# Attention output with stationary values on four column strips, in a fused AdaLN, attention and mixture kernel

## The reference

```python
Q = (X @ Wq).reshape(n, s, NUM_GROUPS, HEADS_PER_GROUP, KEY_WIDTH)
K = (X @ Wk).reshape(n, s, NUM_GROUPS, KEY_WIDTH)
V = (X @ Wv).reshape(n, s, NUM_GROUPS, VALUE_WIDTH)
raw = jnp.einsum('bsgwe,btge->bstgw', Q, K * scale)
attn = jax.nn.softmax(raw, axis=2)
A = jnp.einsum('bstgw,btge->bsgwe', attn, V).reshape(n, s, NUM_HEADS * VALUE_WIDTH)
P = A @ Wpost
return X + P
```

## Time and profile before

| quantity | value |
|---|---|
| median of 3 runs | 577.44 us (577.16 to 578.15) |
| the profiled execution's own time | 579.19 us |
| its span, first to last instruction | 577.4 us |
| PE busy | 559.4 us (97%) |
| DVE busy | 457.8 us (79%) |
| ACT busy | 390.7 us (68%) |
| POOL busy | 310.5 us (54%) |

### The profile page before, as it was taken

The page is one execution under the profiler, slowest core; times in us unless marked ns, Lnnn a source line. Parts: engine busy times, 40 slices in busy tenths (PEclk is TensorE's granted clock), DMA queues, the critical chain, the costliest instruction groups (busy, mean ns, idle before and its releaser), DMA issues.

```text
span 577.4 us, 14607 instructions
## 1 busy us (share of the span) xinstructions
PE 559.4 (97%) x4408; PEld 475.4 (82%) x4408; DVE 457.8 (79%) x966; ACT 390.7 (68%) x911; POOL 310.5 (54%) x268
## 2 busy tenths in 40 slices
PE   8999999999999999999999999999999998978997
PEld 8888888888888888888888888888888976655664
DVE  4244889898889898989898989898989857862865
ACT  1766777777777777777777777777777535647883
POOL 1102666666666666666666666666666544401950
PEclk9999999999999999999999999999999989989999
DMA  7400000000000000000000000000000000000004
GB/s 239 98 2 2 1 2 2 1 0 0 0 0 0 0 0 0 0 0 0 0 0 0 0 0 0 0 0 0 0 0 0 2 1 0 1 1 2 1 1 145
DMA packets 9367, 7.22 MB, mean 13 GB/s; under 512 B 1088, under 2 KB 8832, under 8 KB 9216
## 3 DMA queue, kind: packets, MB, share of 16 engines
q1 hardware_dynamic: 9344, 6.94, 4.1%
HBM read 4.84 MB, written 2.10 MB: 12 GB/s over the span
## 4 chain that ended last, share of the span: by engine, by line
PE 81%; DVE 8%; ACT 5%; issue 3%; DVEq 1%; POOL 0%; ACTq 0%; POOLq 0%
PE bank_a L692 18%; PE misc L699 10%; PE misc L815 10%; PE bank_t L682 8%; PE bank_s L667 6%; PE misc L706 5%; PE misc L833 3%; PE bank_t L677 3%; PE bank_t L931 3%; PE misc L835 2%; DVE row_max L296 2%; DVE h_max L412 2%; PE bank_s L939 2%; PE misc L939 2%; PE bank_s L807 1%
## 5 line engine op out<-in xcount | busy, mean ns | idle before, releaser
L1346 POOL TENSOR_TENSOR pair<-kx 128x1152 f32<-128x1152 f32 x32 | 82.2, 2568 | 172.5 <-DVE shifted L417 155.7
L692 PE MATMUL bank_a<-v,prob 128*128 128x65 f32 x1024 | 128.7, 274 | 1.2 <-ACT prob L985 0.6
L692 PEld LDWEIGHTS bank_a<-v,prob 128*128 128x128 f32 x1024 | 122.0, 192 | 6.0 <-ACT prob L985 3.0
L1341 POOL TENSOR_TENSOR mix_hi<-mix_hi 128x512 f32<-128x512 f32 (+2 forms) x96 | 116.0, 1208 | 7.5
L296 DVE TENSOR_REDUCE row_max<-bank_s 128x4 bf16<-128x512 f32 x128 | 88.8, 694 | 26.6 <-PE bank_s L667 25.7
L985 ACT ACTIVATE prob<-bank_t 128x512 f32<-128x512 f32 x128 | 68.9, 589 | 8.4 <-PE bank_t L682 6.3
L699 PE MATMUL misc<-yT,wq_sb 128*128 128x128 f32 x512 | 69.8, 279 | 0.8 <-DVE yT L477 0.8
L985 ACT ACTIVATE attT<-misc 128x512 f32<-128x512 f32 x64 | 38.1, 595 | 42.8 <-PE misc L706 42.8
L682 PE MATMUL bank_t<-qT,kT 64*128 64x256 f32 x512 | 66.6, 380 | 0.0
L699 PEld LDWEIGHTS misc<-yT,wq_sb 128*128 128x128 f32 x512 | 62.0, 191 | 4.1 <-DVE yT L477 1.0
L307 DVE TENSOR_TENSOR att<-bank_a,recip_den 128x256 f32<-128x256 f32 x128 | 54.4, 425 | 13.0
(11 more groups left out here) (178 smaller groups left out, 989.1 us busy)
## 6 DMA issues: line engine op xcount, KB each, us to landing
out<-acc_all SPq DMA_DIRECT2D x8, 256.0 KB, 2.3
x_all<-in_xT SPq DMA_DIRECT2D x1, 1024.0 KB, 8.9
w_sb<-in_w SPq DMA_DIRECT2D x2, 512.0 KB
x_all<-in_xT SPq DMA_DIRECT2D x1, 768.0 KB, 6.8
wq_sb<-in_wq SPq DMA_DIRECT2D x1, 512.0 KB, 4.9
wpost_sb<-in_wpost SPq DMA_DIRECT2D x1, 512.0 KB, 9.6
x_all<-in_xT SPq DMA_DIRECT2D x1, 256.0 KB, 3.4
b_rows<-in_b SPq DMA_DIRECT2D x16, 4.0 KB
```

The costliest lines, as they stand in the source:

```text
L692: last = mm(att_bank(g)[:, w, :], prob[:, g % 2, w, :], v1[:, j, g, :], start=(w == 0), stop=True, skip_group_check=True)
L1341: G.tensor_tensor(mix_hi[:, jd, 0:r, :], mix_hi[:, jd, 0:r, :], mix_hi[:, jd, r:2 * r, :], ALU.add).then_inc(s_hi, 1)
L1346: G.tensor_tensor(pair[:, :, :], bass.AP(kx2, jc * 2 * P, [[4 * P, P], [0, SHIFTS], [1, P]]), bass.AP(kx2, jc * 2 * P, [[4 * P, P], [MD, S ...
```

## The change

The roles in stage B are exchanged. The values become stationary, 32 columns of them at a time, and the exponentials move, 512 columns (4 heads x 128 queries) in one matmul. The four groups g write to the four 32-partition strips of one bank, which are four column strips of the array. Two such rounds (`attend(s, j, part)`) give the two halves of the 64 values in `bank_a[0]` and `bank_a[1]`, transposed as the post projection wants them. A third round with 32 columns of ones gives the denominators in a new bank `bank_d`, copied over the 32 partitions of each strip. VectorE inverts them in one instruction of 512 columns and multiplies twice with 512 columns, straight into `attT`. The 16 narrow matmuls, the 8 transposes, the two copies by ScalarE, the 4 short reciprocals and the 4 products of 256 columns go away. `prob` gets four buffers in place of two. One bank less is left for `misc`, so other results move to other banks. The rows of Wpost are permuted on the way in.

Other edits come with it. The sum over eight rows of `mix_lo`, which was three additions (L450, L459, L461), becomes one reduction of 1024 to 128 columns, as in the drain before (L514). The order of the instructions of a slot is new on TensorE, VectorE and ScalarE: the fourth `heads_max` of a batch moves into the same slot as the other three, and the post projection is split in two halves, each issued when its half of `attT` is there.

```diff
-        prob = sb("prob", [P, 2, HPG, P])
-        recip_den = sb("recip_den", [P, 2, HPG])
-        att = sb("att", [P, HEADS, KEY])
+        prob = sb("prob", [P, GROUPS, HPG, P])
+        inv_den = sb("inv_den", [P, HPG, P])
...
+        bank_d = pb("bank_d", [P, HPG, P])
+        misc = [pb(f"misc{i}", [P, QUAD, P]) for i in range(2)]
...
-            def invert(s, g):
-                dve.wait_ge(s_av_mm, 4 * s + g + 1)
-                need(dve, s_att, 4 * s + g - 1)
-                V.reciprocal(recip_den[:, g % 2, :].unsqueeze(2), att_bank(g)[:, :, KEY:KEY + 1]).then_inc(s_rden, 1)
...
+            def invert_den(s):
+
+                dve.wait_ge(s_den_mm, n(s))
+                need(dve, s_attT, 2 * s)
+                V.reciprocal(inv_den[:, :, :], bank_d[:, :, :]).then_inc(s_rden, 1)
+
+            def normalise(s, part):
+
+                dve.wait_ge(s_av_mm, 2 * s + part + 1)
+                dve.wait_ge(s_rden, n(s))
+                need(dve, s_post_mm, s)
+                V.tensor_tensor(attT[:, HPG * part:HPG * (part + 1), :],
+                                bank_a[part][:, :].rearrange("p (w q) -> p w q", q=P), inv_den[:, :, :],
+                                ALU.mult).then_inc(s_attT, 1)
...
+                def row_sum():
+                    dve.wait_ge(s_lo, 4 * d + 1)
+                    V.tensor_reduce(mix_part[:, :], mix_lo[:, :, :].rearrange("p r f -> p f r"), AX.X,
+                                    ALU.add).then_inc(s_lo, 3)
...
+            def denominators(s):
+
+                pe.wait_ge(s_prob, 4 * n(s))
+                for g in range(GROUPS):
+                    rows = slice(32 * g, 32 * (g + 1))
+                    last = mm(bank_d[rows, :, :], ones[:, 0:32], prob[:, g, :, :], start=True, stop=True,
+                              skip_group_check=True)
+                last.then_inc(s_den_mm, 1)
+
+            def attend(s, j, part):
+
+                for g in range(GROUPS):
+                    rows = slice(32 * g, 32 * (g + 1))
+                    last = mm(bank_a[part][rows, :], v[:, j, g, 32 * part:32 * (part + 1)],
+                              prob[:, g, :, :], start=True, stop=True, skip_group_check=True)
                 last.then_inc(s_av_mm, 1)
...
+            def posts(b, part):
+
+                pe.wait_ge(s_attT, 2 * b + part + 1)
+                for k in range(4 * part, 4 * part + 4):
+                    last = mm(bank_d[:, 0, :], wpost_sb[:, k, :], attT[:, k, :],
+                              start=(k == 0), stop=(k == CHUNKS - 1))
+                if part == 1:
+                    last.then_inc(s_post_mm, 1)
```

More of the change, by code:

```diff
@@ L156, in build, with key_out, mix_out @@
         bank_a = [pb(f"bank_a{i}", [P, 512]) for i in range(2)]
-        misc = [pb(f"misc{i}", [P, QUAD, P]) for i in range(3)]
+        bank_d = pb("bank_d", [P, HPG, P])
+        misc = [pb(f"misc{i}", [P, QUAD, P]) for i in range(2)]
         bank_x = [b[:, :].rearrange("p (t f) -> p t f", f=P) for b in bank_a] + [misc[1][:, :, :]]
-        bank_e = [bank_s, misc[2]]
+        bank_e = [bank_s, bank_d]
         bank_b = bank_x[0:2] + [misc[0][:, :, :], misc[1][:, :, :]]
-        def att_bank(g):
-            return bank_a[g % 2][:, 0:HPG * (KEY + 1)].rearrange("p (w e) -> p w e", e=KEY + 1)
+        def key_out(b):
+            return misc[1][:, 0:1, :] if s_is(b, BATCH - 1) else bank_x[1][:, 0:1, :]
+        def mix_out(b):
+            return bank_d[:, 0, :] if isinstance(b, int) and b >= BATCH - 3 else misc[1][:, 0, :]
         s_ld_mod, s_ld_modw, s_ld_x0, s_ld_x, s_ld_qkv = (sem("ld_mod"), sem("ld_modw"), sem("ld_x0"),
@@ L448, in loop_slot @@
-                    if D:
[L449 to L461, removed]
@@ L793, in slot @@
-                if s_is(s, BATCH - 1):
-                    gate_logits(parts_early[1])
-                if s_is(s, BATCH):
-                    pe.wait_ge(s_neg, BATCH)
-                    pe.wait_ge(s_rt, ROUTE_STEPS["count1"])
-                    mm(bank_s[:, 0, 0:EXPERTS], ones[:, :], count[:, :], start=True, stop=True).then_inc(s_cnt1_mm, 1)
-                if A:
-                    if C:
-                        pe.wait_ge(s_attT, 2 * c + 1)
-                    need(pe, s_q, 2 * a)
-                    queries(a, 1)
@@ L850, in slot, with keys, keys_turned @@
[L850 to L854 removed]
+                final = s_is(s, BATCH - 1)
+                def keys(b):
+                    pe.wait_ge(s_x1s, n(b))
+                    mm(key_out(b)[:, 0, :], modw_sb[:, 1, :], x1s[:, :], start=True, stop=True).then_inc(s_kx_mm, 1)
+                def keys_turned(b):
+                    pe.wait_ge(s_kxT, n(b))
+                    nc.tensor.transpose(key_out(b)[:, 0, :], kxT[:, :], ident[:, :]).then_inc(s_kxn_mm, 1)
@@ L855, in slot, with drain_slot @@
+                def drain_slot():
+                    if s == BATCH:
+                        posts(c, 0)
+                        posts(c, 1)
+                        keep_going(6)
+                        pick()
+                        pe.wait_ge(s_ld_ffn, 16 * (3 + P // EXPERTS))
+                        ahead_hidden(0)
+                        pe.wait_ge(s_tok, d)
+                        keys(c)
+                        ahead_hidden(1)
+                        keys_turned(c)
                         pe.wait_ge(s_x1T, n(c))
-                    if s_is(s, BATCH):
@@ L857, in slot @@
                         ahead(0, 1, 2)
-                    if s_is(s, BATCH + 1):
+                        mixing_turned(d)
+                        ahead(3)
+                        tokens_made(d)
+                    if s == BATCH + 1:
                         ahead(4, 5, 6)
-                    if s_is(s, BATCH + 2):
+                        mixing_turned(d)
+                        ahead(7)
+                        tokens_made(d)
+                    if s == BATCH + 2:
                         ahead(8)
@@ L906, in slot @@
-                if s_is(s, BATCH + 2):
-                    ahead_hidden(11)
-                    gate_logits(RECENT[-1:])
-                    ahead(10, 11)
+                        mixing_turned(d)
+                        ahead_output(9)
+                        tokens_made(d)
+                        ahead_hidden(11)
+                        gate_logits(RECENT[-1:])
+                        ahead(10, 11)
+                if isinstance(s, int) and s >= BATCH:
+                    drain_slot()
+                else:
+                    loop_slot()
```

384 lines of the change are left out of this document (171 added, 213 removed).

## The result

The changed kernel takes 722.2 us (median of 4 runs, 721.5 to 724.0) against 577.8 us: the ratio is 1.248, 95% interval [1.245, 1.252]. The forecast was 697 us in a range of 648 to 740: the direction and the mechanism hold, and the clock's term is too small. The narrower range that the forecast gave its own mechanism, 675 to 720 us, is missed by 2 us.

What follows compares the result with a forecast made beforehand. A circle through TensorE and VectorE was taken to bound each slot at 17.0 us: 577.4 + 81 (28 slots) + 2 (slots 1 and 2) + 36 (lowered clock) = 696.4 us of span, a median of 697 us, range 648 to 740.

Steps and rivals of the forecast that it cites:

- the mechanism: Per slot, a path through TensorE and VectorE longer than either's work, plus TensorE's lowered clock; 675 to 720 us, chance 0.63.
- the clock's term: TensorE's wait for `yT` each slot lowers its clock to 1.2 GHz afterwards: 1.3 us a slot, 36 us over 28 slots.
- The reciprocal: VectorE's new 512-column inverse of the denominators, priced by extending the line of four narrower ones: 3.35 us, bounds 0.69 and 4.0.
- the row sum: VectorE's single reduction replacing three additions in the loop, priced from the drain's instruction: 1.94 us, bounds 1.35 and 1.96.
- The strips: TensorE's rounds of four column-strip matmuls, taken to run side by side: 1.13 us a round, at most 4.2.
- TensorE's work: Per slot, narrow matmuls and transposes go (5.2 us), three rounds come (3.4 us), leaving about 12.3 us.
- The circle: From `yT` through TensorE to the first row maximum, then VectorE to the next `yT`: 17.0 us a slot, against 14.08.
- first slots: Slots 1 and 2, which have no row sum or mixing, were given 1 us each.
- The waits: Per slot, TensorE idles about 4.7 us, mostly for `yT`; VectorE some 2 us, for `post` and the first scores.
- rival 1: TensorE's clock stays at 2.4 GHz in the loop, so the circle alone remains: 660 us, chance 0.23.
- Rival 2: TensorE's strips don't run side by side: 4.2 us a round, 785 us; two by two 690 to 720; chance 0.10.
- Rival 3: VectorE's wide reciprocal runs at other instructions' rate: at 0.69 us a 14.3 us circle, no change within 1%; chance 0.04.

Runs made afterwards that it cites:

- The kernel at a full clock: Against the changed kernel, twelve matmuls whose result nobody reads fill TensorE's wait for `yT` at the end of its slot: 659.4 us, 1.138 of the kernel before.

## Why the prediction came out as it did

- **The reciprocal (forecast 3.35 us): right**, 3.347. The products (0.69; 0.686) and the row sum (1.94; 1.97) were right as well. That the reciprocal causes the loss is shown from three sides: a quarter of it, none of it on VectorE, and it alone in the kernel before.
- **The strips (1.13 us a round): right**, 0.99 to 1.07 us. TensorE's work was put at 12.3 us a slot; full of work it takes 13.0. What goes was priced by busy time (4.0 + 1.2 us), which counts the end of each group though the next instruction has started; by starts it is 3.6 + 1.0. The rounds were 0.4 us cheaper than forecast, and the other matmuls cost 0.6 us more in the new order, among them the scores (1.14 us in place of 0.90) and the mixture's product (0.40 in place of 0.22).
- **The circle (6.91 + 10.03 + 0.05 = 17.0 us): right within 0.3 us.** With the clock at full speed VectorE's row maximum starts at 313.27, 7.03 us behind the queries at 306.24, and the slot is 16.7 us. TensorE's part was forecast at 6.91 us; VectorE's was forecast at 10.03 and is 9.67. The 81 + 2 us of circle and first slots became 659.3 - 577.4 = 81.9 us between the spans. But two errors hide in that: the slots gave 31 x (16.68 - 14.16) = 78 us, the time up to the first residual addition 6.1 us (I gave it no term), the end -2.3 us. That the total comes so close to 83 is luck.
- **The clock (1.3 us a slot, bounds 0 and 1.7, 36 us): wrong in size.** It is the term that failed, with 63 us measured. The step at fault is "In such a stretch half of the work is lost, 3.4 x 0.49 = 1.7 us", which took the low stretch of the earlier trace rows for the most that a slot can have. In every second slot it was 6.8 us long. The trace of before couldn't show that: its other low stretch in the middle of the work, from 467.3 to 470.7 us, is 3.4 us long, too (and has no wait of more than 0.3 us in the 3 us ahead of it, so a long wait isn't all that brings one about). Two slots have 3.4 + 6.8 = 10.2 us at half speed, at most 10.2 x 0.5 / 2 = 2.5 us a slot; 2.0 were lost. My upper bound was the bound of one length. The missed 27 us are the whole error, 722 - 697 = 25 (the sum itself gives 696: 698.2 / 1.003).
- **The waits.** VectorE's were forecast at 2 us a slot and are 1.90 + 1.11 and 2.81 + 1.10. At full clock they are 0.39 + 1.11: most of the excess is TensorE's slow stretch, seen from VectorE. TensorE's were forecast at 4.7 us a slot; they are 2.8 to 2.9 us for `yT` and some 0.6 us for two copies by ScalarE, as its work is longer and the circle a little shorter than forecast.
- **The rivals.** The kernel at a full clock ran at 659 us, where rival 1 had 660; it was a right sum with a condition that didn't hold. Rival 2 (strips one by one, 785 us) is refuted by the rounds. Rival 3 (a cheap reciprocal) is refuted in its premise. Its sum is borne out in part: with 0.95 us of reciprocal the slot was 14.3 us, the circle that the forecast gave for 0.69. A further one isn't in the list, and wasn't tried: `yT` could stand ahead of the reciprocal on VectorE, since ScalarE has written its input by 313.50 in the slot shown, and the reciprocal starts at 315.36. The post projection behind the queries would still wait for the reciprocal, so what this order is worth is open.
- **What I left out:** the weighting product on VectorE went from 1.51 us to 2.42 (median, 2.55 above). It lies beside TensorE's part of the circle, and VectorE still waits behind it (0.39 us at full clock), so it costs nothing here. In the kernel with the inverse on ScalarE it is 1.24 us, by its median. It overlaps with different work of GpSimd in each; whether that is the cause wasn't tried.

## What to carry to other kernels

Price a wide instruction by its own kind in the trace: two or more widths of it give the line, and a reciprocal is not a copy. Then walk the circle through the engines in their program order, since busy time alone would have allowed a slot of 16.5 us for a spare reciprocal that made it 19.8. When an edit opens a wait on TensorE in each slot, don't take the low clock of one example for the most that it can cost; filling the wait tells its price in one run. And when an improvement has no effect (the strips, the order of the keys), move the bound first: the same edits were worth 5% once the inverse was on ScalarE.

## What the runs showed of the hardware

- VectorE's reciprocal costs 3.347 us for 512 fp32 columns, from PSUM, and 3.35 us from SBUF as well (the spare one), 0.95 us for 128. The line held over more than five times its length.
- ScalarE needs 0.58 us for the logarithm of the 512 columns and 0.63 us for the exponential, together little more than a third of that.
- Four strips of 32 columns, with 512 moving fp32 columns and two passes each, take 1.0 us together.
- Behind a wait of 2.8 to 2.9 us in each slot the granted clock fell to 1.2 GHz for 3.4 and for 6.8 us by turns, so that equal slots took 18.2 and 19.3 us; behind waits of 2.25 to 2.4 us it fell for 3.4, 3.4 and 6.8 us by turns, and with waits of 0.5 us it stayed at 2.4 GHz.
